# A graph network layer: layer 2 of the nodes computed with features on partitions, from layer 1's output split in two

## The chip, the cores and the metric

The kernel runs on one core of one Trainium2 chip. The metric is the device time of the whole program in microseconds (us), as the median of several runs. The engines are PE (TensorE, matrix products), DVE (VectorE), ACT (ScalarE), POOL (GpSimd) and SP (SyncE, which here only issues DMAs). Each runs its own instructions in program order and waits for the others by semaphores.

## The reference

There are 50000 nodes and 25000 edges, both with 128 features. Node rows are normalised and rectified to h. Each edge sends `[h[src], h[dst], edge features]` through a two-layer network (hidden width 256), the results are summed over the edges of each receiver, and each node sends `[h, sum]` through a second two-layer network whose output is added to x.

```
h = jnp.maximum(_layernorm(x, axis=-1), 0.0)
rel_inputs = jnp.concatenate([h[senders], h[receivers], relations], axis=-1)
rel_effects = relu(rel_inputs @ re_w1 + re_b1) @ re_w2 + re_b2
agg_effects = jax.ops.segment_sum(rel_effects, receivers, num_segments=h.shape[0])
effect_inputs = jnp.concatenate([h, agg_effects], axis=-1)
out = x + relu(effect_inputs @ ea_w1 + ea_b1) @ ea_w2 + ea_b2
```

The encoder with the weights oe_w1 and oe_w2 has no influence on the output, and the kernel leaves it out.

## The kernel before

Edges and nodes are worked in groups of 512 (G = 4 x 128, T = 4). There are 49 groups of edges, and 98 tiles of nodes that go in 49 pairs; r = 1 and r = 2 are the two tiles of a pair, j is the pair, e the group of edges. Edges come sorted by receiver, so the sum for a tile of nodes needs only a window of 128 edge results for each 128 nodes. The edges run three groups ahead of the nodes: three edge steps, then `enter`, then 46 joint steps (one group of edges and one pair of nodes each, e = 3 to 48, j = e - 3), then three pair steps with nodes alone.

A joint step does this. DVE takes statistics of the gathered rows of the next edge group and of the next x tiles (L726, L731), turns them into a scale and a shift (L738 to L758, with a square root by ACT in between, `deviations`), and normalises the edges' rows with eight 128x128 instructions (`normalise_edges`, L767); ACT normalises the nodes' rows (`normalise`, L638). PE transposes them to features on partitions (`turn_edges`, `turn_nodes`), and sums a window of edge results with a 0/1 matrix `hot` (`sum_window`), which DVE makes from the window (`mark`, L807). Everything that enters layer 1 is split in a high part, rounded to fp32r by ACT (`high_ea`, `high_edges`, `high_nodes`), and a low part, value minus high part, by DVE (`low_edges`, `low_features`, `low_sums`) or, for the edge features, by POOL (`low_ea`, L397). Layer 1 then takes for each of its two halves c of 128 hidden units the products high x w_high, high x w_low and low x w_high, as fp32r matmuls with 512 columns (L514, L519). ACT adds the bias and rectifies (`hidden`, L630). Layer 2 (L529) multiplies in plain fp32: for each of the four blocks of 128 rows, the hidden block stands still and the weights of 128 columns are moved through, twice, so the output has rows on partitions. DVE adds the bias and writes the edge results (`edge_results`), or adds `xb` = x + bias, which POOL has made (`keep_x`, L390), and writes the node results (`node_results`, L801). POOL also issues the gathers of the edges' rows: eight indirect DMAs a group (L374). SP loads windows, edge features and x tiles and stores the results.

The order on each engine is written out by hand in `joint_step` and `pair_step` of each engine's block; semaphores (`wait_ge`) hold an instruction until its inputs are there. The buffers l1_ps, l2_ps, node_ps and agg_ps are PSUM banks, the others lie in SBUF.

## Time and profile before

| | us |
|---|---|
| median of 3 runs | 969.56 (969.46 to 970.05) |
| the profiled execution, device time | 968.67 |
| its span (first to last instruction) | 966.9 |
| PE busy | 938.2 |
| DVE busy | 674.7 |
| POOL busy | 577.2 |
| ACT busy | 553.1 |

The profile is one execution. The span is 1.8 us shorter than the device time of the same execution, and the median of the runs is 0.9 us above that device time. In a row of a timeline the first number is the start from the span's begin, the second the duration, both in us; "x8" says that eight instructions stand in the row; the brackets say how long the engine had been idle before it and what ended that.

### The profile page before, as it was taken

The numbers are of one execution on the slowest core, as the hardware profiler recorded it, in microseconds if no ns is written. First come the engines' busy times: TensorE is split into PE (matmuls) and PEld (weight loads), VectorE is DVE, ScalarE is ACT, GpSimd is POOL, SyncE is SP. The second block draws the span as 40 slices with busy tenths as digits, with TensorE's granted clock in tenths as the row PEclk, the third lists the DMA queues.
The fourth block names the chain that finished last, engine by engine and source line by source line (L and its number), as shares of the span: only waits on it lengthen the run. The fifth ranks groups of instructions, "written<-read, shape, count | busy, mean of one in ns | idle before, by whom it ended". The sixth has DMA issues, their size and how long they took to land.

```text
span 966.9 us, 20070 instructions
## 1 busy us (share of the span) xinstructions
PE 938.2 (97%) x6058; PEld 834.2 (86%) x6058; DVE 674.7 (70%) x2057; ACT 553.1 (57%) x1082; POOL 577.2 (60%) x600
## 2 busy tenths in 40 slices
PE   4879999999999999999999999999999999999997
PEld 3668988998898898899889889988988998898886
DVE  5876776777677677767767776776776677677552
ACT  1356556556655655665565666566566556655653
POOL 7777666665665666566566656656665665662220
PEclk9999999999999999999999999999999999999999
DMA  6354444454544545454454545545444544543332
GB/s 197 91 130 114 138 139 137 144 145 133 159 144 133 143 143 146 131 158 143 131 151 143 142 129 156 146 128 164 134 143 125 157 144 129 164 138 117 109 91 70
DMA packets 114100, 132.51 MB, mean 137 GB/s; under 512 B 17984, under 2 KB 70080, under 8 KB 113984
## 3 DMA queue, kind: packets, MB, share of 16 engines
q1 hardware_dynamic: 101440, 105.43, 36.3%
q0 software_dynamic: 12544, 25.72, 10.6%
q8 instruction: 51, 0.84, 0.4%
q14 instruction: 65, 0.53, 0.2%
HBM read 92.07 MB, written 39.00 MB: 136 GB/s over the span
## 4 chain that ended last, share of the span: by engine, by line
PE 93%; DVE 4%; issue 1%; ACT 1%; DMA 0%; POOL 0%; SPq 0%; DVEq 0%; POOLq 0%
PE l_ps L514 32%; PE l_ps L529 27%; PE l_ps L519 16%; PE agg_ps L483 9%; PE edge_ps L467 4%; PE node_ps L475 4%; PE node_ps L459 1%; DVE h L767 1%; DVE st L726 1%; DVE st L731 0%; DVE hot L807 0%; DVE lo L774 0%; DMA gath<-in_x,dst_all 0%; DMA drow_i<-in_dst_rows 0%; POOL gath L374 0%
## 5 line engine op out<-in xcount | busy, mean ns | idle before, releaser
L374 POOL DMA_INDIRECT gath<-in_x,dst_all x196 | 193.6, 988 | 59.9 <-issue 59.9
L374 POOL DMA_INDIRECT gath<-in_x,src_all x196 | 188.1, 960 | 52.2 <-issue 45.8
L780 DVE SCALAR_TENSOR_TENSOR lo<-node_ps,hi 128x512 fp32r<-128x512 f32 x98 | 67.8, 692 | 202.7 <-ACT hi L621 202.7
L397 POOL TENSOR_TENSOR ea_lo<-ea_in,ea_hi 128x512 fp32r<-128x512 f32 x45 | 63.1, 1401 | 217.0 <-ACT ea_hi L612 217.0
L529 PE MATMUL l_ps<-w2n,hid 128*128 128x128 f32 x1568 | 190.9, 275 | 0.0
L529 PEld LDWEIGHTS l_ps<-w2n,hid 128*128 128x128 f32 x1568 | 183.0, 192 | 0.1
L630 ACT ACTIVATE hid<-l_ps,b1n 128x512 f32<-128x512 f32 x196 | 135.3, 690 | 81.9 <-PE l_ps L519 81.7
L638 ACT ACTIVATE h<-xin,shift,rs 128x128 f32<-128x128 f32 x392 | 165.0, 483 | 0.0
L514 PE MATMUL l_ps<-hi,w1n_hi 128*128 128x512 f32 x392 | 155.8, 398 | 0.6 <-ACT hid L630 0.6
L514 PE MATMUL l_ps<-hi,w1n_lo 128*128 128x512 f32 x392 | 155.4, 396 | 0.0
L390 POOL TENSOR_TENSOR xb<-xin,b2n 128x512 f32<-128x512 f32 x98 | 124.5, 1292 | 33.2 <-DVE res L801 33.2
L621 ACT ACTIVATE hi<-node_ps 128x512 fp32r<-128x512 f32 x98 | 58.2, 594 | 138.4 <-PE node_ps L475 138.2
L630 ACT ACTIVATE hid<-l_ps,b1e 128x512 f32<-128x512 f32 x98 | 67.7, 691 | 108.0 <-PE l_ps L519 108.0
L519 PE MATMUL l_ps<-lo,w1n_hi 128*128 128x512 f32 x392 | 123.6, 396 | 0.0
L483 PE MATMUL agg_ps<-hot,win 128*128 128x128 f32 x784 | 104.8, 277 | 3.6 <-DVE hot L807 3.4
L767 DVE TENSOR_SCALAR h<-gath,rs,shift 128x128 f32<-128x128 f32 x392 | 105.7, 344 | 1.8
L483 PEld LDWEIGHTS agg_ps<-hot,win 128*128 128x128 f32 x784 | 96.1, 193 | 4.7 <-issue 4.1
L529 PE MATMUL l_ps<-w2e,hid 128*128 128x128 f32 x784 | 95.9, 275 | 2.3 <-ACT hid L630 2.3
L529 PEld LDWEIGHTS l_ps<-w2e,hid 128*128 128x128 f32 x784 | 91.4, 192 | 3.6 <-ACT hid L630 3.6
L514 PEld LDWEIGHTS l_ps<-hi,w1n_hi 128*128 128x128 f32 x392 | 74.0, 189 | 19.2 <-ACT hid L630 1.4
L519 PEld LDWEIGHTS l_ps<-lo,w1n_hi 128*128 128x128 f32 x392 | 73.6, 188 | 18.2
L514 PEld LDWEIGHTS l_ps<-hi,w1n_lo 128*128 128x128 f32 x392 | 73.9, 189 | 17.4
(94 smaller groups left out, 1441.8 us busy)
## 6 DMA issues: line engine op xcount, KB each, us to landing
win<-rel_rows SPq DMA_DIRECT2D x392, 66.0 KB
xin<-in_x_tiles SPq DMA_DIRECT2D x98, 256.0 KB, 4.1
out<-res SPq DMA_DIRECT2D x98, 256.0 KB, 3.3
rel_rows<-rel_row SPq DMA_DIRECT2D x49, 264.0 KB
ea_in<-in_ea_t SPq DMA_DIRECT2D x49, 256.0 KB, 3.1
gath<-in_x,src_all POOLq DMA_INDIRECT x196, 2.7
gath<-in_x,dst_all POOLq DMA_INDIRECT x196, 2.6
w1e<-in_L_gnn_re_w SPq DMA_DIRECT2D x1, 384.0 KB
```

What stands on the lines that cost most here:

```text
L374: nc.gpsimd.indirect_dma_start(gath[b][:, s, k, :], None, x, bass.IndirectOffsetOnAxis(ap=idx[:, e * T + k:e * T + k + 1], axis=0)).then_i ...
L390: nc.gpsimd.tensor_tensor(xb[r][j % 2][:, :, :], xin[r][j % 3][:, :, :], b2[1][:, :].unsqueeze(1).to_broadcast([P, T, D]), ALU.add).then_i ...
L397: nc.gpsimd.tensor_tensor(ea_lo[e % 2][:, :], ea_in[e % 2][:, :], ea_hi[e % 2][:, :].bitcast(F32), ALU.subtract).then_inc(ea_lo_set, 1)
L483: last = nc.tensor.matmul(agg_ps[:, k * P:(k + 1) * P], win[r][:, k, 0:D], hot[r][:, k, :], start=True, stop=True)
L514: nc.tensor.matmul(l1_ps[c][:, :], part[:, q, c * P:(c + 1) * P], high, start=(i == 0 and part is w1hi[w]), stop=False)
L519: last = nc.tensor.matmul(l1_ps[c][:, :], w1hi[w][:, q, c * P:(c + 1) * P], low, start=False, stop=(i == len(srcs) - 1))
L529: last = nc.tensor.matmul(l2_ps[turn % 2][:, k * P:(k + 1) * P], hid[r][:, c, k * P:(k + 1) * P], w[:, c, :], start=(c == 0), stop=(c == C ...
L621: nc.scalar.activation(hi[r][:, 0, :], node_ps[:, :], ACT.Relu).then_inc(node_hi_set, 1)
L630: nc.scalar.activation(hid[r][:, c, :], l1_ps[c][:, :], ACT.Relu, bias=b[:, c:c + 1]).then_inc(hid_set, 1)
L638: last = nc.scalar.activation(h[r][:, k, :], xin[r][j % 3][:, k, :], ACT.Identity, bias=shift[j % 2][:, b:b + 1], scale=rs[j % 2][:, b:b + 1])
L767: last = nc.vector.tensor_scalar(h[0][:, s * T + k, :], gath[e % 2][:, s, k, :], rs[e % 2][:, t:t + 1], shift[e % 2][:, t:t + 1], ALU.mult ...
L780: nc.vector.scalar_tensor_tensor(out=lo[r][:, 0, :], in0=node_ps[:, :], scalar=0.0, in1=hi[r][:, 0, :].bitcast(F32), op0=ALU.max, op1=ALU. ...
```

## The change

Layer 2 of the nodes changes its form. The weights w2n stand still (128x128, one for each half c) and the hidden tile of 512 columns is moved through, so the output has features on partitions and 512 nodes as columns. It is done in split form, as layer 1 is. w2n and the hidden tile are split in high and low parts, and six fp32r matmuls of 512 columns take the place of eight plain fp32 ones of 128. ACT makes `hid_hi` with two copies a tile (`high_hidden`), POOL makes `hid_lo` with two subtractions a tile (`low_hidden`). The residual comes from a transposed copy of x, `x_t`, which SP loads for each tile (`load_xt`); the bias is now one number a partition, and `node_results` adds both in one instruction. `keep_x` and `xb` go. The output is stored in the transposed layout. x is still loaded in rows, for the statistics and the normalisation. Once, at the start, DVE splits w2n (`split_last_weights`). The order of the joint step changes on PE, ACT, DVE and POOL.

```diff
+            def layer2_nodes(r, j, turn):
+                wait(pe, results, turn - 1)
+                for c in range(C):
+                    pe.wait_ge(hid_hi_set, C * tile_no(r, j) + c + 1)
+                    nc.tensor.matmul(l2_ps[turn % 2][:, :], w2hi[:, c, :], hid_hi[r][:, c, :], start=(c == 0), stop=False)
+                    nc.tensor.matmul(l2_ps[turn % 2][:, :], w2lo[:, c, :], hid_hi[r][:, c, :], start=False, stop=False)
+                for c in range(C):
+                    pe.wait_ge(hid_lo_set, C * tile_no(r, j) + c + 1)
+                    last = nc.tensor.matmul(l2_ps[turn % 2][:, :], w2hi[:, c, :], hid_lo[r][:, c, :], start=False, stop=(c == C - 1))
```

The order of a joint step on PE:

```diff
             def joint_step(e, j):
-                for r, n in ((0, e), (1, j), (2, j)):
-                    for c in range(C):
-                        layer1(r, n, turn + r, c)
-                if j + 1 < NJ:
-                    turn_nodes(1, j + 1)
-                    sum_window(1, j + 1)
+                for r, n, c in ((0, e, 0), (0, e, 1), (1, j, 0), (1, j, 1), (2, j, 0)):
+                    layer1(r, n, turn + r, c)
+                turn_nodes(1, j + 1)
+                layer1(2, j, turn + 2, 1)
+                layer2(turn)
+                layer2_nodes(1, j, turn + 1)
                 if e + 1 < EG:
                     turn_edges(e + 1)
-                layer2(0, turn)
-                layer2(1, turn + 1)
-                if j + 1 < NJ:
-                    turn_nodes(2, j + 1)
-                    sum_window(2, j + 1)
-                layer2(2, turn + 2)
+                sum_window(1, j + 1)
+                layer2_nodes(2, j, turn + 2)
+                turn_nodes(2, j + 1)
+                sum_window(2, j + 1)
```

The new work of POOL:

```diff
+            def low_hidden(r, j):
+                for c in range(C):
+                    pool.wait_ge(hid_hi_set, C * tile_no(r, j) + c + 1)
+                    nc.gpsimd.tensor_tensor(hid_lo[r][:, c, :], hid[r][:, c, :], hid_hi[r][:, c, :].bitcast(F32),
+                                            ALU.subtract).then_inc(hid_lo_set, 1)
```

The new work of ACT, and its joint step as it stands now:

```diff
+            def hidden_nodes(r, j, turn, c):
+                act.wait_ge(l1_done, C * turn + c + 1)
+                wait(act, hid_lo_set, C * tile_no(r, j - 1) + c + 1)
+                nc.scalar.activation(hid[r][:, c, :], l1_ps[c][:, :], ACT.Relu, bias=b1[1][:, c:c + 1]).then_inc(hid_set, 1)
+
+            def high_hidden(r, j, turn, c, before):
+                act.wait_ge(hid_set, C * turn + c + 1)
+                if c == 0:
+                    wait(act, l2_done, before + 1)
+                nc.scalar.activation(hid_hi[r][:, c, :], hid[r][:, c, :], ACT.Copy).then_inc(hid_hi_set, 1)
...
             def joint_step(e, j):
+                normalise(1, j + 1, True)
                 if e + 1 < EG:
                     high_ea(e + 1, True)
+                hidden(turn, 0, before_edge(e, True))
+                hidden(turn, 1, before_edge(e, True))
+                hidden_nodes(1, j, turn + 1, 0)
+                deviations(e + 1, some(e + 1, EG), pair_of(e + 1))
+                hidden_nodes(1, j, turn + 1, 1)
+                for c in range(C):
+                    high_hidden(1, j, turn + 1, c, before_node(1, j, True))
+                hidden_nodes(2, j, turn + 2, 0)
+                high_features(1, j + 1)
+                high_hidden(2, j, turn + 2, 0, before_node(2, j, True))
+                hidden_nodes(2, j, turn + 2, 1)
+                high_hidden(2, j, turn + 2, 1, before_node(2, j, True))
+                normalise(2, j + 1, True)
                 if e + 1 < EG:
                     high_edges(e + 1)
+                high_sums(1, j + 1, True)
+                high_features(2, j + 1)
+                high_sums(2, j + 1, True)
```

The results of the nodes on DVE:

```diff
             def node_results(r, j, fast):
...
-                dve.wait_ge(xb_set[r], j + 1)
+                dve.wait_ge(xt_loaded[r][j % 3], 16 * (j // 3 + 1))
                 wait(dve, stored[r], 16 * j)
-                nc.vector.tensor_tensor(res[r][:, :, :], tiled(l2_ps[turn % 2]), xb[r][j % 2][:, :, :], ALU.add).then_inc(results, 1)
+                nc.vector.scalar_tensor_tensor(out=res[r][:, :], in0=l2_ps[turn % 2][:, :], scalar=b2[1][:, 0:1],
+                                               in1=xt[r][j % 3][:, :], op0=ALU.add, op1=ALU.add).then_inc(results, 1)
```

The order on POOL in one joint step before: after the eight gathers (the last of them is the first row), the low part of the next edge features, then x plus bias for both tiles of the next pair, then the marks of the edges' receivers (COPY) and the next gathers.

```order
L374 DMA gath<-in_x,dst_all 128x128
L397 TENSOR_TENSOR ea_lo<-ea_in,ea_hi 128x512 [waits ea_hi_set]
L390 TENSOR_TENSOR xb<-xin,b2n 128x512 [waits results,x_loaded12]
L390 TENSOR_TENSOR xb<-xin,b2n 128x512 [waits results,x_loaded22]
L384 COPY rel_row<-dst_f 128x4 [waits rel_stored0]
L374 DMA gath<-in_x,src_all 128x128 [waits normed0]
```

And the same place now.

```order
L396 DMA gath<-in_x,dst_all 128x128
L418 TENSOR_TENSOR ea_lo<-ea_in,ea_hi 128x512 [waits ea_hi_set]
L411 TENSOR_TENSOR hid_lo<-hid,hid_hi 128x512 [waits hid_hi_set] x4
L406 COPY rel_row<-dst_f 128x4 [waits rel_stored0]
L396 DMA gath<-in_x,src_all 128x128 [waits normed0]
```

Two additions for the next pair have become four subtractions for this pair, and each waits for ACT's `hid_hi`.

The order on DVE in the second part of one joint step before, from the scale and shift to the last low part.

```order
L801 TENSOR_TENSOR res<-l_ps,xb 128x512 [waits stored2,xb_set2,l2_done]
L756 RECIPROCAL rs<-sd 128x16 [waits deviation]
L758 SCALAR_TENSOR_TENSOR shift<-total,rs 128x16 [waits inverse]
L767 TENSOR_SCALAR h<-gath,rs,shift 128x128 [waits edges_turned,shift_set]
L767 TENSOR_SCALAR h<-gath,rs,shift 128x128 x7
L807 SCALAR_TENSOR_TENSOR hot<-node_no,win 128x512 [waits win_used1,win_loaded1]
L780 SCALAR_TENSOR_TENSOR lo<-node_ps,hi 128x512 [waits node_hi_set]
L785 TENSOR_TENSOR lo<-agg_ps,hi 128x512 [waits agg_hi_set]
L774 SCALAR_TENSOR_TENSOR lo<-edge_ps,hi 128x512 [waits edge_hi_set] x2
L793 TENSOR_TENSOR rel_row<-l_ps,b2e 128x4x128 [waits l2_done,rel_stored0]
L807 SCALAR_TENSOR_TENSOR hot<-node_no,win 128x512 [waits win_used2,win_loaded2]
```

And the same part now.

```order
L797 RECIPROCAL rs<-sd 128x16 [waits deviation]
L799 SCALAR_TENSOR_TENSOR shift<-total,rs 128x16 [waits inverse]
L849 SCALAR_TENSOR_TENSOR hot<-node_no,win 128x512 [waits win_used1,win_loaded1,shift_set]
L842 SCALAR_TENSOR_TENSOR res<-l_ps,b2n,xt 128x512 [waits stored2,xt_loaded21,l2_done]
L808 TENSOR_SCALAR h<-gath,rs,shift 128x128 [waits edges_turned]
L808 TENSOR_SCALAR h<-gath,rs,shift 128x128 x7
L849 SCALAR_TENSOR_TENSOR hot<-node_no,win 128x512 [waits win_used2,win_loaded2]
L834 TENSOR_TENSOR rel_row<-l_ps,b2e 128x4x128 [waits l2_done,rel_stored0]
L821 SCALAR_TENSOR_TENSOR lo<-node_ps,hi 128x512 [waits node_hi_set]
L842 SCALAR_TENSOR_TENSOR res<-l_ps,b2n,xt 128x512 [waits stored1,xt_loaded12,l2_done]
L815 SCALAR_TENSOR_TENSOR lo<-edge_ps,hi 128x512 [waits edge_hi_set] x2
L826 TENSOR_TENSOR lo<-agg_ps,hi 128x512 [waits agg_hi_set]
```

Both `hot` have moved: the first in front of the eight normalisations, the second right behind them, and the results and all low parts of the step stand behind that.

## Rows read from the trace of the kernel before

**Rows 1.** Windows, one joint step: length; PE, PEld, DVE, ACT, POOL busy; clock; DMA.
```profile
477.67:496.40 18.73, 18.73 (x125) 16.76 (x124) 13.42 (x43) 11.24 (x23) 11.82 (x13) 1.00 0.49 142
```
**Rows 2.** The chain that ended last, in that step: start, us, what.
```profile
482.13 0.94 PE l_ps L514 x4
...
487.75 0.44 PE node_ps L475 x4
488.19 0.89 PE agg_ps L483 x8
489.08 0.87 PE edge_ps L467 x8
489.95 3.57 PE l_ps L529 x32
```
**Rows 3.** Groups by line and form: busy us, mean ns of one, idle before.
```profile
L397 POOL TENSOR_TENSOR ea_lo<-ea_in,ea_hi 128x512 fp32r<-128x512 f32 x45 | 63.1, 1401 | 217.0 <-ACT ea_hi L612 217.0
...
L612 ACT ACTIVATE ea_hi<-ea_in 128x512 fp32r<-128x512 f32 x49 | 30.6, 626 | 2.7 <-DMA ea_in<-in_ea_t 2.7
...
L834 DVE TENSOR_TENSOR w1e_lo<-w1e,w1e_hi 128x768 fp32r<-128x768 f32 x1 | 1.0, 959 | 0.0
...
L832 DVE CAST w1e_hi<-w1e 128x768 fp32r<-128x768 f32 x1 | 0.6, 550 | 0.0
```
**Rows 4.** Timelines of that step, PE, ACT, DVE and POOL.
```profile
482.36 2.14 DVE L767 TENSOR_SCALAR h<-gath,rs,shift 128x128 f32<-128x128 f32 x8
...
483.37 0.39 PE L514 MATMUL l_ps<-hi,w1n_hi 128*128 128x512 f32 x1
...
483.57 0.69 ACT L630 ACTIVATE hid<-l_ps,b1n 128x512 f32<-128x512 f32 x1
...
484.86 1.39 POOL L397 TENSOR_TENSOR ea_lo<-ea_in,ea_hi 128x512 fp32r<-128x512 f32 x1 [4.64 <-ACT ea_hi L612]
...
486.22 2.53 POOL L390 TENSOR_TENSOR xb<-xin,b2n 128x512 f32<-128x512 f32 x2
...
489.02 1.00 POOL L374 DMA_INDIRECT gath<-in_x,src_all  x1
...
490.62 1.29 DVE L774 SCALAR_TENSOR_TENSOR lo<-edge_ps,hi 128x512 fp32r<-128x512 f32 x2 [0.18 <-ACT hi L617]
...
492.82 1.15 POOL L374 DMA_INDIRECT gath<-in_x,dst_all  x1 [0.30 <-issue]
```
**Rows 5.** Timelines of the first pair step: the square root and a DVE instruction after it.
```profile
928.50 0.30 ACT L606 ACTIVATE sd<-spread,eps 128x8 f32<-128x8 f32 x1 [1.48 <-DVE spread L750]
...
929.27 0.69 DVE L801 TENSOR_TENSOR res<-l_ps,xb 128x512 f32<-128x512 f32 x1
```
**Rows 6.** Timelines where POOL and DVE both work on SBUF tiles (behind `enter`; pair step).
```profile
56.56 2.50 POOL L390 TENSOR_TENSOR xb<-xin,b2n 128x512 f32<-128x512 f32 x2
...
57.70 1.91 DVE L807 SCALAR_TENSOR_TENSOR hot<-node_no,win 128x512 f32<-128x512 f32 x1
...
59.00 0.66 POOL L384 COPY rel_row<-dst_f 128x4 f32<-128x4 f32 x1
...
930.11 1.29 POOL L390 TENSOR_TENSOR xb<-xin,b2n 128x512 f32<-128x512 f32 x1 [4.44 <-DVE res L801]
...
930.82 1.12 DVE L807 SCALAR_TENSOR_TENSOR hot<-node_no,win 128x512 f32<-128x512 f32 x1 [0.85 <-DMA win<-rel_rows]
```
**Rows 7.** Instructions of one line: ns min/median/max, first and last start.
```profile
L767 DVE TENSOR_SCALAR h<-gath,rs,shift x392: 331/343/566, 20.3 to 896.3; 128x128 f32<-128x128 f32 x196
...
L801 DVE TENSOR_TENSOR res<-l_ps,xb x98: 683/692/692, 81.4 to 962.4; 128x512 f32<-128x512 f32 x98
...
L807 DVE SCALAR_TENSOR_TENSOR hot<-node_no,win x98: 677/682/1910, 57.7 to 949.4; 128x512 f32<-128x512 f32 x98
```
**Rows 8.** Just behind `enter`: a PE timeline row, and a window (columns as rows 1).
```profile
58.62 0.90 PE L475 MATMUL node_ps<-ident,h 128*128 128x128 f32 x4 [2.79 <-ACT h L638]
...
60.00:62.00 2.00, 2.00 (x11) 2.00 (x11) 0.69 (x1) 0.72 (x3) 1.70 (x2) 0.50 0.14 33
```

More of the change, by code:

```diff
@@ L113, in gnn_program @@
         xin = [None] + [[sb(f"xin{r}{b}", [P, T, D]) for b in range(3)] for r in (1, 2)]
-        xb = [None] + [[sb(f"xb{r}{b}", [P, T, D]) for b in range(2)] for r in (1, 2)]
+        xt = [None] + [[sb(f"xt{r}{b}", [P, G]) for b in range(3)] for r in (1, 2)]
+        hid_hi = [None] + [sb(f"hid_hi{r}", [P, C, G], F32R) for r in (1, 2)]
+        hid_lo = [None] + [sb(f"hid_lo{r}", [P, C, G], F32R) for r in (1, 2)]
         win = [None] + [sb(f"win{r}", [P, T, ROW]) for r in (1, 2)]
         hot = [None] + [sb(f"hot{r}", [P, T, P]) for r in (1, 2)]
-        res = [None] + [sb(f"res{r}", [P, T, D]) for r in (1, 2)]
+        res = [None] + [sb(f"res{r}", [P, G]) for r in (1, 2)]
         edge_ps = [ps(f"edge_ps{s}", [P, G]) for s in range(2)]
@@ L320, in _ @@
                     load_x(r, j)
+            for r in (1, 2):
+                load_xt(r, 0, True)
             def edge_step(e, last, fast):
@@ L343, in joint_step @@
                 for r in (1, 2):
+                    if j + 1 < NJ:
+                        load_xt(r, j + 1, True)
+                for r in (1, 2):
                     if j + 3 < NJ:
@@ L354, in pair_step @@
                     store(2, j - 1, fast)
+                for r in (1, 2):
+                    if j + 1 < NJ:
+                        load_xt(r, j + 1, fast)
                 for r in (1, 2):
@@ L427, in edge_step @@
                     gather(e + 2)
-                if last:
-                    pool.wait_ge(loaded[1], LOADS)
-                    for r in (1, 2):
-                        keep_x(r, 0, fast)
                 if FIRST < e + 1 < EG:
@@ L592, in pair_step @@
                     add(1, j + 1)
-                layer2(1, turn)
+                layer2_nodes(1, j, turn)
                 if j + 1 < NJ:
@@ L705, in pair_step @@
                     deviations(stats_turn(j + 2, fast), None, j + 2)
-                hidden(1, turn, 0, before_node(1, j, fast))
-                hidden(1, turn, 1, before_node(1, j, fast))
+                for c in range(C):
+                    hidden_nodes(1, j, turn, c)
+                    high_hidden(1, j, turn, c, before_node(1, j, fast))
                 if more:
                     normalise(2, j + 1, fast)
-                hidden(2, turn + 1, 0, before_node(2, j, fast))
-                hidden(2, turn + 1, 1, before_node(2, j, fast))
+                for c in range(C):
+                    hidden_nodes(2, j, turn + 1, c)
+                    high_hidden(2, j, turn + 1, c, before_node(2, j, fast))
                 if more:
@@ L894, in _ @@
             split_weights(1)
+            split_last_weights()
             def edge_step(e, last, fast):
@@ L923, in joint_step @@
                 spreads(*what)
+                invert(*what)
+                mark(1, j + 1)
                 if j > 0:
                     node_results(2, j - 1, True)
-                invert(*what)
                 if e + 1 < EG:
                     normalise_edges(e + 1, range(T))
-                if more:
-                    mark(1, j + 1)
-                    low_nodes(1, j + 1)
+                mark(2, j + 1)
+                edge_results(e, True)
+                low_features(1, j + 1)
+                node_results(1, j, True)
                 if e + 1 < EG:
                     low_edges(e + 1)
-                edge_results(e, True)
-                if more:
-                    mark(2, j + 1)
-                node_results(1, j, True)
-                if more:
-                    low_nodes(2, j + 1)
+                low_sums(1, j + 1)
+                low_nodes(2, j + 1)
             def pair_step(j, fast):
```

96 lines of the change are left out of this document (43 added, 53 removed).

## The prediction

> **What bounds the kernel now.** I read the windows first. In a joint step of the middle, PE is busy for 18.73 of 18.73 us, DVE for 13.42, ACT for 11.24, POOL for 11.82, and PE's granted clock is 1.00, which is 2.4 GHz [rows 1]. So PE sets the end, and 46 such steps make 862 of the 966.9 us. The chain that ended last says what PE does in it: a layer 1 matmul of 512 columns comes every 0.94 / 4 = 0.235 us, and layer 2 of two tiles of nodes takes 3.57 us, 1.79 a tile [rows 2]. The timelines then say what leaves room: POOL had been idle for 4.64 us before `low_ea`, and DVE's eight normalisations, begun at 482.36 and 2.14 us long, were over at 484.50, before POOL's first subtraction of the step began at 484.86 [rows 4]. In this kernel the two do not meet; that will matter.
>
> **What PE saves.** Layer 2 of a tile of nodes becomes six matmuls of 512 columns. Layer 1 has the same shape and type, so I take 6 x 0.235 = 1.41 us, 0.38 less than 1.79. A joint step becomes 18.73 - 0.75 = 17.98 us, if nothing waits. With nothing else, 98 tiles would give 37 us.
>
> **What the other engines get.** ACT gets four copies from SBUF of 0.63 us, priced by `high_ea` [rows 3]: 11.24 + 2.5 = 13.8 us, below 17.98. DVE gets nothing: the new `node_results` reads one PSUM and one SBUF tensor of 512, as the old one did at 0.69 [rows 7]. POOL loses two `xb` (2.53 together) and gets four subtractions of the form of `low_ea`, 1.39 in that step and 1.40 in the mean [rows 3, 4]. Its step was three gathers in 492.82 - 489.02 = 3.80 us, so 1.27 each; eight are 10.2, the COPY about 0.3, five subtractions 7.0, together 17.5 us. That is under 17.98, but only just. SP gets two more loads of the size of those of x a step; the 16 DMA engines are busy for 0.49 of the time [rows 1], and a fifth more bytes leave them under 0.6. I take 0 for it, as the loads are issued a step ahead. At the start `split_last_weights` adds two small DVE instructions, about 0.6 us, and the additions of `keep_x` that held up DVE's first `hot` (1.91 instead of 0.68 us [rows 6, 7]) go, 1.2 us: together -0.6.
>
> **Where the work now stands in a step.** I lay the new order out from t = 0, PE's first matmul of the step, with 0.235 a matmul and the 0.44, 0.87 and 0.89 of [rows 2]. PE: both halves of layer 1 of the edges end at 4.2, tile 1 at 5.6 and 7.0, tile 2's half 0 at 8.5, transposes 8.9, half 1 at 10.3, layer 2 of the edges 12.1, of tile 1 at 13.5, `turn_edges` 14.4, window sum 15.3, layer 2 of tile 2 at 16.7, transposes 17.1, window sum 18.0. ACT starts on a result 0.20 after PE has gone on [483.57 against 483.37, rows 4]: `hidden_nodes` of tile 1, half 0, at 5.8, then the square root at 6.4, half 1 at 7.25, `high_hidden` at 7.85, done at 8.5. The later `hid_hi` are done by my count at 9.1, 10.8 and 12.1. POOL, whose gathers and `low_ea` are over by about 7.9, therefore subtracts at 8.5, 9.9, 11.2, 12.6, back to back until 14.0. DVE: 0.77 us after the start of the square root it is free for the next instruction [rows 5], so `hot` of tile 1 at 7.2, `node_results` of tile 2 at 7.8 and the eight normalisations from 8.4 (instructions of 512 follow each other every 0.60, the pair of 1.29 less one of 0.69 [rows 4, 7]). Unhindered they end at 10.5, three us before PE wants them at 13.5. **They now fall upon POOL's four subtractions.**
>
> **What such a meeting costs.** `hot`, which reads two SBUF tensors, met an `xb` of POOL twice. At 57.70 it took 1.91 us instead of 0.68 and ended at 59.61, 0.55 behind the end of POOL's pair at 59.06; at 930.82 it took 1.12 and ended at 931.94, 0.54 behind POOL's end [rows 6]. Streaming 512 elements takes about that, so DVE did not start until POOL had finished: one waits for the whole instruction of the other. It is mutual: the COPY of 0.2 us issued at 59.00 took 0.66. `node_results`, which has one input in PSUM, was never above 0.692 [rows 7]. The normalisation has one SBUF input and an SBUF output. A cast of such a form does 768 elements in 0.55 us where a subtraction of two tensors takes 0.96 [rows 3], so this form moves twice as many in the same time and must use both of DVE's ways into SBUF. And while its median is 343 ns, one took 566 [rows 7], during a gather's index read. I therefore take it that it waits for a subtraction as `hot` does. Its price lies between nothing (its longest delay shown is 0.22) and the whole subtraction each time POOL has one.
>
> A page gives the rule: the Trainium skill, SBUF — State Buffer, section "Who interferes with whom", says that a DVE instruction in a two-port mode (a tensor_scalar can run so) or with two SBUF inputs and a GpSimd instruction exclude each other for whole instructions. For `hot` the trace agrees (1.91 and 1.12 us); for the normalisation no row has the meeting.
>
> **The sum.** One normalisation slips in at the end of each subtraction, which the COPY's turn at 59.06 speaks for. Four are then done when POOL ends, at about 14.3 with the hand-overs; four more at 0.26 lead to 15.4. Behind them stand in order the second `hot`, `edge_results`, `low_features`, `node_results`, two `low_edges` and `low_sums`: the seventh starts 6 x 0.60 later, at 19.0, and ends at 19.7. PE's last window sum waits for it, since agg_ps has to be read before: 19.8 to 20.7, and with the restart 20.8 us a step. PE's own waits are about 1.3 us at `turn_edges` and 1.5 before that last sum. The excess is 20.8 - 18.73 = 2.07 us in each of the 45 steps that still normalise edges, 93 us. The last joint step has none: -0.8 for PE, about +1 for a `hot` that waits for POOL, so 0. The three pair steps put four ACT copies of about 0.6 in front of `high_features`, for which PE waits there, and save 0.75: about +1 each for the two with a successor, +2. The start: -0.6. The span is 966.9 + 93 + 2 - 0.6 = 1061.3. The device time was 1.8 longer, and the median 0.9 above that: 1064 us.
>
> **The rivals.** (a) **POOL keeps its turn.** At 57.83, between the two `xb`, the waiting `hot` did not get in. Then no normalisation passes until 14.0, eight end at 16.2, the last low part at 20.5, the step is 21.5: 45 x 2.8 = 125 us, 1096. (b) **Two pass at each hand-over**, as they are pipelined (0.26 apart, 0.34 long): 0.9 us less a step, 1024. (c) **The normalisation does not mind POOL**, on the other side: what decides is whether its form takes POOL's way into SBUF at all. Then DVE is 0.8 us free before each need, the steps are 18.0, and 46 x 0.75 = 34.5 us are gained: 966.9 - 34.5 + 2 - 0.6 + 2.7 = 937. Against it stand the cast's speed and the 566 ns. (d) **DVE goes first and keeps its turn**, starting at 8.4, just before POOL: POOL begins at 11.2, the second `hid_lo` is there at 13.9 where PE wants it at 13.3, and the step is 18.6: 963 to 967. Against it: POOL's index read came in between two normalisations. (e) **The clock.** After a PE idle stretch of 2.79 us the granted clock of the window 60 to 62 was 0.50, 1.2 GHz [rows 8]. If the waits of a step bring that, some 4 us at half speed cost 2 us more a step: about 1155. The new single waits are about half as long, so this is unlikely. (f) The matmuls cost more than in layer 1: same shape, same types, I give it nothing.
>
> **How the numbers follow.** Chances: forecast 0.47, (a) 0.24, (b) 0.09, (c) 0.12, (d) 0.05, (e) 0.03. The cases forecast, (a) and (b) hold 0.80; their range, with 4 us for my rounding, is 1020 to 1100. About 0.2% (2 us) is what a measurement here can tell from no change. Faster: (c) and part of (d), 0.14; within 0.2%: 0.03; slower: 0.83.
>
> **What would show it.** Right: normalisations of some 1.4 us beside subtractions that follow without a gap; PE idle at `turn_edges` and before the second window sum of a step, released by DVE; joint steps of about 20.8 us; layer 2 of a tile at 1.41 us. Wrong: normalisations that keep 0.34 us (then 937), or a clock below 1.00 in joint steps (then far above 1100).

## The result and the profile after

The changed kernel takes **1028.84 us** (median of 4 runs, 1027.49 to 1032.22) where the kernel before, on the same chip, takes 969.51 (968.68 to 970.05). The ratio is 1.0618, with a 95% interval of 1.059 to 1.0646: 6% slower. The forecast was 1064, its range 1020 to 1100. The profiled execution of the changed kernel spans 1025.6 us, 58.7 more than the 966.9 of before.

From the page of the changed kernel: busy times, the chain that ended last, and two groups, in the form of [rows 3].

```profile
PE 933.6 (91%) x5078; PEld 764.8 (75%) x5078; DVE 847.3 (83%) x2059; ACT 644.9 (63%) x1278; POOL 690.5 (67%) x698
...
PE 49%; DVE 32%; issue 15%; ACT 3%; POOL 0%; DMA 0%; DVEq 0%; SPq 0%; POOLq 0%; ACTq 0%
...
L411 POOL TENSOR_TENSOR hid_lo<-hid,hid_hi 128x512 fp32r<-128x512 f32 x196 | 247.2, 1291 | 201.0 <-ACT hid_hi L670 200.5
...
L808 DVE TENSOR_SCALAR h<-gath,rs,shift 128x128 f32<-128x128 f32 x392 | 291.2, 812 | 0.1
```

The normalisation took 344 ns in the mean before (343 in the median [rows 7]) and now takes 812 in the mean, and DVE, which had 4% of the chain before, has 32%. One joint step of the middle, as [rows 1] and with the same columns:

```profile
482.06:502.00 19.94, 18.67 (x105) 15.30 (x104) 17.21 (x41) 13.07 (x26) 14.04 (x14) 1.00 0.56 161
```

18.73 us have become 19.94, at a granted clock of 1.00. The timelines of that step, DVE, POOL and PE, in place of [rows 4]:

```profile
490.64 6.31 DVE L808 TENSOR_SCALAR h<-gath,rs,shift 128x128 f32<-128x128 f32 x8
...
490.64 5.01 POOL L411 TENSOR_TENSOR hid_lo<-hid,hid_hi 128x512 fp32r<-128x512 f32 x4 [3.60 <-ACT hid_hi L670]
...
496.69 0.68 DVE L849 SCALAR_TENSOR_TENSOR hot<-node_no,win 128x512 f32<-128x512 f32 x1
...
500.34 0.67 DVE L826 TENSOR_TENSOR lo<-agg_ps,hi 128x512 fp32r<-128x512 f32 x1
...
494.10 0.47 PE L552 MATMUL l_ps<-hid_hi,w2n_hi 128*128 128x512 f32 x1
...
495.56 1.18 PE L482 MATMUL edge_ps<-ident,h 128*128 128x128 f32 x6
...
497.01 0.44 PE L482 MATMUL edge_ps<-ident,h 128*128 128x128 f32 x2 [0.26 <-DVE h L808]
...
497.29 1.06 PE L498 MATMUL agg_ps<-hot,win 128*128 128x128 f32 x8
...
499.58 0.60 PE L490 MATMUL node_ps<-ident,h 128*128 128x128 f32 x4
...
501.12 1.13 PE L498 MATMUL agg_ps<-hot,win 128*128 128x128 f32 x8 [0.94 <-issue]
```

The first two rows of PE say what the change gave: layer 2 of a tile runs from 494.10 to 495.56, 1.46 us in place of 1.79. The rest says what it took. Eight normalisations last 6.31 us where they lasted 2.14, beside four subtractions of POOL. In the whole run 179 of the 392 normalisations take more than 1.2 us, four in nearly every one of the 45 joint steps that have them. PE stands idle for them at `turn_edges` (0.26 in its row, and more between the transposes that the row merges) and before the step's last window sum (0.94). The profile calls that second wait `issue`; by the code, `sum_window` waits there for the last low part of DVE, which is over at 501.01. Cut into narrower windows, the 6.31 us read so:

```profile
490.64 1.37 DVE L808 TENSOR_SCALAR h<-gath,rs,shift 128x128 f32<-128x128 f32 x1
...
491.93 2.55 DVE L808 TENSOR_SCALAR h<-gath,rs,shift 128x128 f32<-128x128 f32 x2
...
494.41 1.59 DVE L808 TENSOR_SCALAR h<-gath,rs,shift 128x128 f32<-128x128 f32 x2
...
495.66 0.59 DVE L808 TENSOR_SCALAR h<-gath,rs,shift 128x128 f32<-128x128 f32 x2
```

They start at 490.64, 491.93, 493.18 and 494.41, one every 1.25 us, which is the spacing of the subtractions (5.01 / 4). From 495.66, when POOL is done, they come 0.26 apart. Two more rows, of the line of the normalisation (ns min/median/max) and of who waited for it (us, times):

```profile
L808 DVE TENSOR_SCALAR h<-gath,rs,shift x392: 329/524/1389, 20.6 to 954.9; 128x128 f32<-128x128 f32 x196
...
  PEld edge_ps L482: 36.2, 93
```

So PE's weight loads wait 0.8 us a step (36.2 / 45) inside `turn_edges`; the 0.26 of the PE row lies within that. What the two places cost is read from the starts of the rows. `turn_edges` runs from 495.56 to 497.29, 1.73 us, and the last window sum starts 1.54 us behind the start of `turn_nodes` (499.58 to 501.12). The kernel without POOL's subtractions (x3_no_sub, below) has 0.87 and 0.53 us there. The differences, 0.86 and 1.01, and that kernel's step of 18.06 make 19.93: the step.

**Where the 58.7 us lie.** The step of e = 3 starts at 64.20 (before: 64.73), the last joint step at 960.48 (before: 908.53). The start gives back 0.5; 45 steps of 19.92 instead of 18.75 cost 52.5. From there to the last result of DVE it is 57.21 instead of 54.52, +2.7. And behind the last result comes a stretch of 7.9 us instead of 3.9. Of the kernel before and of the one after, the last row of the chain and the row of the instruction with which POOL's queue ends:

```profile
962.36 0.69 DVE L801 TENSOR_TENSOR res<-l_ps,xb 128x512 f32<-128x512 f32 x1 [1.09 <-PE l_ps L529]
```
```profile
L44 POOLq DRAIN  x1: 7667/7667/7667, 944.4 to 944.4; - x1
```
```profile
1016.94 0.75 DVE L842 SCALAR_TENSOR_TENSOR res<-l_ps,b2n,xt 128x512 f32<-128x512 f32 x1 [1.17 <-PE l_ps L556]
```
```profile
L44 POOLq DRAIN  x1: 7666/7666/7666, 1017.7 to 1017.7; - x1
```

POOL's drain takes 7.67 us. Before, it began at 944.4 and was over at 952.1, long before the end. Now POOL works until the last layer 2, the drain begins at 1017.7, and the program ends 0.2 us behind it. That is +4.1 us that the forecast did not have; x11_end_on_dve, below, tests it. -0.5 + 52.5 + 2.7 + 4.1 is 58.8.

### The profile page after: what moved, and what is told of

It is laid out like the page before. It is cut to its first block, busy times and chain, and to the rows that moved or that the text cites. A ratio compares the mean times of both kernels' runs of the same rounds, so it can differ in the third digit from the quotient of the medians.

```text
span 1025.6 us, 18464 instructions
## 1 busy us (share of the span) xinstructions
PE 933.6 (91%) x5078; PEld 764.8 (75%) x5078; DVE 847.3 (83%) x2059; ACT 644.9 (63%) x1278; POOL 690.5 (67%) x698
## 2 busy tenths in 40 slices
DMA packets 128208, 158.05 MB, mean 154 GB/s; under 512 B 19680, under 2 KB 71648, under 8 KB 128096
## 4 chain that ended last, share of the span: by engine, by line
PE 49%; DVE 32%; issue 15%; ACT 3%; POOL 0%; DMA 0%; DVEq 0%; SPq 0%; POOLq 0%; ACTq 0%
DVE h L808 23%; PE l_ps L529 18%; PE agg_ps L498 10%; PE l_ps L534 9%; DVE res L842 3%; PE l_ps L552 2%; PE l_ps L556 2%; PE l_ps L553 2%; PE edge_ps L482 2%; PE node_ps L490 2%; ACT sd L630 1%; DVE rs L797 1%; DVE shift L799 1%; DVE st L772 1%; DVE st L767 1%
## 5 line engine op out<-in xcount | busy, mean ns | idle before, releaser
L411 POOL TENSOR_TENSOR hid_lo<-hid,hid_hi 128x512 fp32r<-128x512 f32 x196 | 247.2, 1291 | 201.0 <-ACT hid_hi L670 200.5
L808 DVE TENSOR_SCALAR h<-gath,rs,shift 128x128 f32<-128x128 f32 x392 | 291.2, 812 | 0.1
L396 POOL DMA_INDIRECT gath<-in_x,dst_all x196 | 185.9, 949 | 59.7 <-issue 59.7
L529 PE MATMUL l_ps<-hi,w1n_hi 128*128 128x512 f32 x392 | 159.7, 407 | 1.8 <-ACT hid L664 1.8
L678 ACT ACTIVATE h<-xin,shift,rs 128x128 f32<-128x128 f32 x392 | 160.6, 482 | 0.0
L826 DVE TENSOR_TENSOR lo<-agg_ps,hi 128x512 fp32r<-128x512 f32 x98 | 66.9, 683 | 64.5 <-ACT hi L653 64.5
L670 ACT ACTIVATE hid_hi<-hid 128x512 fp32r<-128x512 f32 x196 | 118.2, 628 | 1.9
L641 ACT ACTIVATE hi<-edge_ps 128x512 fp32r<-128x512 f32 x98 | 53.2, 595 | 102.2 <-PE edge_ps L482 102.2
L653 ACT ACTIVATE hi<-agg_ps 128x512 fp32r<-128x512 f32 x98 | 59.1, 603 | 74.8 <-PE agg_ps L498 74.8
L482 PE MATMUL edge_ps<-ident,h 128*128 128x128 f32 x392 | 74.3, 292 | 14.1 <-DVE h L808 10.1
```

The source lines that it names most:

```text
L396: nc.gpsimd.indirect_dma_start(gath[b][:, s, k, :], None, x, bass.IndirectOffsetOnAxis(ap=idx[:, e * T + k:e * T + k + 1], axis=0)).then_i ...
L411: nc.gpsimd.tensor_tensor(hid_lo[r][:, c, :], hid[r][:, c, :], hid_hi[r][:, c, :].bitcast(F32), ALU.subtract).then_inc(hid_lo_set, 1)
L482: last = nc.tensor.transpose(edge_ps[s][:, k * P:(k + 1) * P], h[0][:, s * T + k, :], ident[:, :])
L529: nc.tensor.matmul(l1_ps[c][:, :], part[:, q, c * P:(c + 1) * P], high, start=(i == 0 and part is w1hi[w]), stop=False)
L670: nc.scalar.activation(hid_hi[r][:, c, :], hid[r][:, c, :], ACT.Copy).then_inc(hid_hi_set, 1)
L678: last = nc.scalar.activation(h[r][:, k, :], xin[r][j % 3][:, k, :], ACT.Identity, bias=shift[j % 2][:, b:b + 1], scale=rs[j % 2][:, b:b + 1])
```

## The experiments

The theory: DVE's normalisation and POOL's subtraction shut each other out for whole instructions, one normalisation passes at each hand-over, and that chain delays the last low part of the step. The rivals left are that something else of the change (traffic, matmuls, ACT's copies) costs the time, and that the interference follows another rule. Unless something else is said, each kernel is the changed one with the edit shown; the kernel before took 968.96 to 970.49 us beside them.

**Without the subtractions**

```diff
-                for r in (1, 2):
-                    low_hidden(r, j)          # and layer 2 reads hid_hi in the place of hid_lo
```

> The changed kernel without POOL's four subtractions a joint step (and four a pair step); the last two matmuls of layer 2 of a tile read hid_hi in place of hid_lo, so the low part of the hidden tile is left out of the result. PE, ACT, DVE and DMAs keep their order. Theory (DVE's normalisations of the edges wait for POOL's subtractions, one passing per subtraction): the eight normalisations fall from 6.3 us a step to 2.1, joint steps from 19.94 us to about 18.0, the span from 1025.6 to 1025.6 - 45 x 1.95 = 938. Rival (the new order on the engines, or the waits of ACT and PE for one another, make the steps long): normalisations short, but steps still above 19.5 us, span above 1010. Rival (memory traffic of the second copy of x): span unchanged within 3 us.

942.21 us, ratio 0.9721 [0.9701, 0.974]. POOL's subtractions and the waits of PE and ACT for them are the only thing that is left out (the output lacks the low part of the hidden tile). A joint step as in [rows 1], the line of the normalisation, and the PE rows of the two places:

```profile
481.87:499.93 18.06, 18.06 (x105) 15.33 (x104) 13.56 (x42) 13.07 (x26) 9.49 (x11) 1.00 0.60 176
```
```profile
L805 DVE TENSOR_SCALAR h<-gath,rs,shift x392: 328/342/585, 20.3 to 871.6; 128x128 f32<-128x128 f32 x196
```
```profile
495.36 1.04 PE L480 MATMUL edge_ps<-ident,h 128*128 128x128 f32 x8
...
496.23 1.06 PE L496 MATMUL agg_ps<-hot,win 128*128 128x128 f32 x8
...
498.52 0.60 PE L488 MATMUL node_ps<-ident,h 128*128 128x128 f32 x4
...
499.05 1.13 PE L496 MATMUL agg_ps<-hot,win 128*128 128x128 f32 x8
```

The step is 18.06 us, all of it PE, and the normalisation has its 342 ns again. That is 0.08 over the forecast's 17.98, with the matmuls, ACT's copies, the new `res` and the loads all in it: they do not make a joint step longer, and the 1.9 us are the subtractions. It is not PE's wait for `hid_lo` itself either: in the changed kernel PE waits for it once in the whole run, 0.3 us, near the end.

**Without the loads of x_t**

```diff
             def load_xt(r, j, fast):
                 if j > 2:
-                    sp.wait_ge(results, node_turn(r, j - 3, fast) + 1)
+                    return
```

> The changed kernel without the loads of x in the second layout (x_t) from the fourth pair of tiles on: node_results adds old values, and 92 of the 98 loads of 256 KB are left out. It prices the traffic that the change adds. My theory (the step is set by POOL's subtractions and DVE's normalisations between them, the loads are hidden): joint steps stay at 19.9 us, profiled span 1025.6 +- 3 us, time about 1029. The rival (the added bytes slow the gathers, and with them the edges): the steps fall by some tenths of a us, the span to 1020 or below.

1028.54 us (1027.55 to 1029.53), ratio 1.0593 [1.055, 1.0636]. Bytes moved fall from 158.05 to 133.91 MB, the span is 1027.7, and the last window sums of steps start at 901.98, 921.91, 941.84 and 961.78, still 19.93 apart. The traffic is hidden.

**The subtractions cut in two, and joined in pairs**

```diff
-                    nc.gpsimd.tensor_tensor(hid_lo[r][:, c, :], hid[r][:, c, :], hid_hi[r][:, c, :].bitcast(F32), ...
+                    for f in (slice(0, G // 2), slice(G // 2, G)):                       # x4_halves
+                        last = nc.gpsimd.tensor_tensor(hid_lo[r][:, c, f], hid[r][:, c, f], ...
...
-                for c in range(C):                                                           # x5_double, once a tile
+                pool.wait_ge(hid_hi_set, C * tile_no(r, j) + C)
+                nc.gpsimd.tensor_tensor(hid_lo[r][:, :, :], hid[r][:, :, :], ...
```

> The changed kernel with each of POOL's subtractions cut in two of 256 columns. Theory (one normalisation passes at the end of each POOL instruction): eight ends in place of four, so all eight normalisations are through when POOL is; POOL's work grows to about 5.3 us, the second hot starts 5.3 us after the first normalisation and not 6.05, steps of about 19.2 us, span about 990. Rival (a fixed delay by the time that POOL works, whatever the number of its instructions): the second hot starts later by what POOL's work grows, span 1030 to 1045.

> The changed kernel with the two subtractions of a tile made one of 1024 columns. Theory (one normalisation passes at the end of each POOL instruction): the first subtraction starts 0.5 us later, at 9.1 us of the step, so two or three normalisations are through before; it lasts about 2.3 us; four or five remain and the second subtraction starts about 0.4 us behind the first one's end, so about three stay behind it until 14.3 us: second hot at about 15.0 instead of 14.6 us, steps of 20.1 to 20.4 us, span 1030 to 1045. Rival (a fixed price per POOL instruction or per hand-over): half as many of them, steps shorter than now, span below 1010.

1008.4 us (1008.18 to 1008.62), ratio 1.0403 [1.0383, 1.0424], and 1045.61 (1045.38 to 1045.83), ratio 1.0759 [1.072, 1.0799]. The rows of x4_halves, then of x5_double:

```profile
483.07 5.24 DVE L810 TENSOR_SCALAR h<-gath,rs,shift 128x128 f32<-128x128 f32 x8
...
482.63 5.60 POOL L412 TENSOR_TENSOR hid_lo<-hid,hid_hi 128x256 fp32r<-128x256 f32 x8 [2.27 <-ACT hid_hi L672]
...
478.80 1.62 DVE L781 TENSOR_TENSOR total<-st 128x32 f32<-128x32 f32 x1
...
479.06 1.29 POOL L420 TENSOR_TENSOR ea_lo<-ea_in,ea_hi 128x512 fp32r<-128x512 f32 x1
```
```profile
479.58 5.50 DVE L807 TENSOR_SCALAR h<-gath,rs,shift 128x128 f32<-128x128 f32 x5
...
479.40 2.51 POOL L410 TENSOR_TENSOR hid_lo<-hid,hid_hi 128x1024 fp32r<-128x1024 f32 x1 [3.88 <-ACT hid_hi L669]
...
482.27 2.47 POOL L410 TENSOR_TENSOR hid_lo<-hid,hid_hi 128x1024 fp32r<-128x1024 f32 x1 [0.36 <-ACT hid_hi L669]
```

The same elements are subtracted in all three. With halves the price of a normalisation is that of one instruction of POOL: 5.24 / 8 = 0.66 us beside 5.60 / 8 = 0.70. With double ones, the individual normalisations show one held for 2.41 us beside each of POOL's two instructions, and six that pass before, between and behind them (between them POOL waits 0.36 us for ACT). So each instruction of POOL holds one normalisation for its whole length, long or short. The eight together last 6.27 us, no more than with single ones; that fewer and longer subtractions lengthen the chain is not shown. The steps of x5_double alternate between 20.07 and 20.51 us, with the second `hot` at 14.75 and 15.20 us of the step, where the changed kernel has 14.63.

Part of both results is another meeting: `total`, a DVE instruction of 0.20 us on two small SBUF tiles, met `low_ea` and took 1.62 us. It did so in nearly every step of x4_halves and in every other step of x5_double, the longer ones, and it delays the first normalisation, to 9.0 us of the step instead of 8.6. That is what was off for the halves, where I wanted steps of 19.2 us and a span of about 990: the second `hot` came 5.16 us behind the first normalisation, for 5.3 forecast, but the steps were 19.50 us and the span 1006.7.

**The subtractions on DVE**

```diff
+                low_hidden(1, j)              # now in DVE's code, ahead of edge_results
                 edge_results(e, True)
+                low_hidden(2, j)
                 low_features(1, j + 1)
```

> The changed kernel with the four subtractions of the hidden tile done by DVE in place of POOL (0.6 us each there, 2.4 us a step). Theory: DVE has 13.4 + 2.4 = 15.8 us of work in a step of 18.0, and nothing of POOL meets the normalisations but low_ea, which ends before; steps of 18.0 to 18.5 us, span 938 to 962. Rival (DVE is the engine that is short, whoever delays it): DVE's chain from the square root to low_sums is 1.2 to 2.4 us longer than without the subtractions, so steps of 18.8 to 19.8, span 975 to 1020.

955.97 us (954.94 to 957.49), ratio 0.9868 [0.9851, 0.9884]. With nobody on the other side, the rows of a step have 2.13 us for eight normalisations and 1.29 for two subtractions, which follow each other every 0.6 us on DVE, where POOL needs 1.25. Steps are about 18.3 us; DVE's longer queue holds up the last sum by 0.22.

**The square root and the normalisations early (x1_early)**

```diff
+                deviations(e + 1, some(e + 1, EG), pair_of(e + 1))    # ACT, ahead of hidden_nodes(1, j, turn + 1, 0)
                 invert(*what)
+                if e + 1 < EG:
+                    normalise_edges(e + 1, range(T))                  # DVE, ahead of mark and node_results
                 mark(1, j + 1)
```

> The changed kernel with the edges' normalisations moved out of the way: ACT takes the square root before hidden_nodes of tile 1, half 0, and DVE normalises the edges before hot and node_results. Nothing is left out, POOL's four subtractions stay. Theory: the normalisations start about 6.4 us into the step and end at 8.5, where POOL begins; hot of tile 2 waits for one subtraction at most, with no one waiting for it; steps of 18.0 to 18.3 us, span 938 to 952, so faster than the kernel before. Rival (POOL's subtractions slow the step for another reason, as that POOL has no time left: its step was counted at 17.3): steps of 19 us or more, span 980 or more.

1048.8 us (1045.7 to 1049.38), ratio 1.0822 [1.0804, 1.084]: a miss, and slower than the changed kernel. Every other step is as expected, 18.05 us (471.10 to 489.15). The one after it takes 22.87:

```profile
489.15:512.02 22.87, 19.91 (x106) 16.66 (x104) 18.82 (x42) 13.18 (x26) 18.44 (x19) 0.93 0.49 139
```
```profile
495.26 1.61 DVE L799 SCALAR_TENSOR_TENSOR shift<-total,rs 128x16 f32<-128x16 f32 x1
...
495.53 1.30 POOL L418 TENSOR_TENSOR ea_lo<-ea_in,ea_hi 128x512 fp32r<-128x512 f32 x1
...
496.91 6.14 DVE L808 TENSOR_SCALAR h<-gath,rs,shift 128x128 f32<-128x128 f32 x8
...
497.72 4.99 POOL L411 TENSOR_TENSOR hid_lo<-hid,hid_hi 128x512 fp32r<-128x512 f32 x4 [0.89 <-ACT hid_hi L670]
...
504.36 0.77 PE L552 MATMUL l_ps<-hid_hi,w2n_hi 128*128 128x512 f32 x1 [2.96 <-DVE res L842]
```

`shift`, 16 columns wide and 0.17 us long by itself, met `low_ea` and took 1.61. The normalisations, late by that, fell on the subtractions after all; `node_results` stood behind them, and PE waited 2.96 us for the free PSUM bank and went on at a lower granted clock (0.93 in the mean of the step). An order with a margin of a microsecond failed on the smallest instruction in it.

**The same, with low_ea behind the subtractions (x8_early_ea_last, and once more as x8_again)**

```diff
-                if e + 1 < EG:
-                    low_ea(e + 1)
                 for r in (1, 2):
                     low_hidden(r, j)
+                if e + 1 < EG:
+                    low_ea(e + 1)
```

> x1_early with one more change: POOL makes the low part of the next edge features behind the four subtractions of the hidden tiles and not ahead of them (PE wants it 1.6 us into the next step). Nothing is left out. Theory (x1 failed because shift, a DVE instruction with two SBUF inputs, met low_ea and took 1.61 us, which pushed the normalisations back into the subtractions): shift and the normalisations now fall in a stretch where POOL has no tensor instruction, shift takes 0.2 and the eight normalisations 2.1 to 2.4 us, the first starts at 6.5 us of the step; steps of 18.0 to 18.3 us, span 938 to 952. Rival (x1 was slow because hot and node_results came later, for which PE waited, or because POOL has no time left): steps above 19.5 us, span above 1000.

946.3 us (945.48 to 947.4), ratio 0.9741 [0.9712, 0.977].

```profile
479.72:497.79 18.07, 18.07 (x106) 15.34 (x104) 13.93 (x42) 13.19 (x26) 14.80 (x15) 1.00 0.58 176
```
```profile
485.83 0.18 DVE L799 SCALAR_TENSOR_TENSOR shift<-total,rs 128x16 f32<-128x16 f32 x1
...
486.05 2.14 DVE L808 TENSOR_SCALAR h<-gath,rs,shift 128x128 f32<-128x128 f32 x8
...
488.30 5.82 POOL L411 TENSOR_TENSOR hid_lo<-hid,hid_hi 128x512 fp32r<-128x512 f32 x4 [0.98 <-ACT hid_hi L670]
```

One move on POOL beside x1_early makes 102 us: `shift` has its 0.18, the normalisations 2.14 and are over 0.1 before POOL begins, and every step is PE's 18.07. All of the new layer 2 is kept here, subtractions on POOL included: the loss was one of order, not of work. This version beats both kernels.

**DVE with the subtractions and the early square root (x9_dve_early)**

```diff
 x2_on_dve, and:
+                deviations(e + 1, some(e + 1, EG), pair_of(e + 1))    # ACT, as in x1_early
+                high_features(1, j + 1)       # ACT, pair step, ahead of the copies of tile 2
```

> x2_on_dve (subtractions of the hidden tiles on DVE) with the square root ahead of hidden_nodes of tile 1 on ACT, and in the pair steps the high features of tile 1 ahead of the copies of tile 2. Nothing is left out. Theory: DVE's chain starts 0.9 us earlier, so the last low part is there before PE's last window sum wants it; steps go from 18.3 to about 18.0 us, 46 x 0.25 = 11 us, and the pair steps give 1 to 2 us: span 938 to 942. Rival (x2 was bound by POOL or DMA): unchanged within 3 us of 953.

954.91 us (953.16 to 956.34), ratio 0.982 [0.9789, 0.9851], where I wanted 938 to 942. A miss: the step stays at 18.28, because the square root is not what DVE's last low part hangs on.

```profile
480.91 0.69 DVE L836 TENSOR_TENSOR rel_row<-l_ps,b2e 128x512 f32<-128x512 f32 x1 [0.86 <-PE l_ps L534]
...
496.69 2.48 POOL L396 DMA_INDIRECT gath<-in_x,dst_all  x1 [0.30 <-issue]
```

`edge_results` waits 0.86 us for PE, and seven instructions of 0.6 stand behind it. The second row is a gather, otherwise 0.94, that met two subtractions of DVE.

**The pair steps of the best version (x10_best)**

```diff
                 for c in range(C):
                     hidden_nodes(2, j, turn + 1, c)
+                if more and fast:
+                    high_features(1, j + 1)
+                for c in range(C):
                     high_hidden(2, j, turn + 1, c, before_node(2, j, fast))
```

> The version with the square root early, the normalisations ahead of hot and node_results and low_ea behind the subtractions, and in the pair steps ACT's high_features of tile 1 ahead of the copies of tile 2's hidden layer. In the changed kernel PE waited 1.78 us for ACT in the first pair step, and a pair step took 13.95 us instead of 13.1 to 13.4. Only the two pair steps with a successor can gain: joint steps 18.07 us as without the tweak, pair steps about 13.0 us, so 1 to 2 us less than 946.3: 944 to 946 us, ratio to the kernel before 0.973. Rival: PE waits next for something else in those steps (the copies of tile 2, which now end later), and the time stays at 946 to 947.

946.77 us (945.41 to 948.84), ratio 0.9758 [0.9729, 0.9787]: no change, as the rival had it. PE's waits of 1.39 for ACT and 1.27 for `hot` in the first pair step become one of 2.33 for `hot`, since `low_sums`, ahead of `hot` on DVE, now waits for ACT's later copy.

**The end of the program**

```diff
             def pair_step(j, fast):           # POOL, in x8_early_ea_last
+                if j < NJ - 1:
                     for r in (1, 2):
                         low_hidden(r, j)      # those of the last pair go to DVE, behind node_results(2, j - 1)
```

> The version with the square root early, the normalisations ahead of hot and node_results and low_ea behind the subtractions, once more, beside the next kernel on the same chip. Its profile had DVE's last result at 935.85 and its end at 943.7 us: 7.85 us behind it, where the kernel before has 3.85 (963.05 and 966.9). I expect 945 to 947 us again.

> The same version with the four subtractions of the last pair of tiles on DVE, which is idle for 6.24 us there. Theory: what lies behind the last result is POOL's DRAIN at the end of the program, which takes 7.67 us from the moment POOL's queue is empty; in the kernel before it begins at 944.4 and is hidden, in the changed kernel and in this version it begins at DVE's last result, since POOL's last subtraction ends just before. With the last subtractions on DVE, POOL is done one pair step earlier: the drain begins before 922 us, the stretch behind the last result falls from 7.85 to 3.9 to 4.3 us, and PE's wait of 0.25 us for the last hid_lo goes. Span 939.5 +- 0.7, time 941.5 to 943, some 4 us below the run beside it. Rival: the stretch is the store of out in its new layout (128 rows of 2 KB), or the profile's own; then it stays at 7.9 us and the time falls by at most 0.5 us.

947.42 us (947.29 to 948.63) without the edit and **943.28** (941.48 to 943.58) with it, on the same chip; ratios to the kernel before 0.9771 [0.975, 0.9792] and 0.972 [0.9698, 0.9742]. Drain and last result, without and with:

```profile
L44 POOLq DRAIN  x1: 7667/7667/7667, 937.6 to 937.6; - x1
```
```profile
936.79 0.75 DVE L842 SCALAR_TENSOR_TENSOR res<-l_ps,b2n,xt 128x512 f32<-128x512 f32 x1 [1.16 <-PE l_ps L556]
```
```profile
L44 POOLq DRAIN  x1: 7688/7688/7688, 925.0 to 925.0; - x1
```
```profile
935.71 1.55 DVE L849 SCALAR_TENSOR_TENSOR res<-l_ps,b2n,xt 128x512 f32<-128x512 f32 x2
```

The stretch behind the last result falls from 945.5 - 937.54 = 8.0 us to 941.2 - 937.26 = 3.9. The drain it was; the store in its new layout, which both have, costs nothing. This is the fastest version tried, 2.8% below the kernel before.

**The other way round: the kernel before with an early high_ea (x6_before_early_ea)**

```diff
+                if e + 1 < EG:
+                    high_ea(e + 1, True)      # ACT, in the kernel before, ahead of hidden(0, turn, 0, ...)
                 hidden(0, turn, 0, before_edge(e, True))
```

> The kernel before with one instruction moved: ACT makes ea_hi of the next edges ahead of hidden of the edges, so POOL's low_ea and its two xb follow its gathers at once and fall beside DVE's normalisations. Theory: the normalisations, 0.34 us each at present, take up to 1.3 us there, the eight together 3.3 to 5 us instead of 2.1, as POOL's xb (no hidden tile, no new layout) hold them up too; PE wants them 6 us later, so the span stays within 2 us of 966.9. Rival (only the new subtractions or the new order lengthen them): eight in 2.1 to 2.3 us.

It was to bring the old `xb` upon the normalisations and got 975.42 us (973.49 to 977.57), ratio 1.0045 [1.0025, 1.0066]. In the steady steps it missed: the normalisations kept 2.14 us, what was hit was `shift`, and PE did not notice (18.73 us). At the start it met them once. The profiled span is 975.5 us, 8.6 more than before where I wanted at most 2, and nearly all of that lies there: the step of e = 3 starts at 69.41 (before: 64.73) and takes 22.95 us (before: 19.55). Rows of a steady step, then of the start:

```profile
490.91 1.27 DVE L758 SCALAR_TENSOR_TENSOR shift<-total,rs 128x16 f32<-128x16 f32 x1
...
490.86 1.28 POOL L390 TENSOR_TENSOR xb<-xin,b2n 128x512 f32<-128x512 f32 x1 [1.34 <-DVE res L801]
...
56.32 4.03 DVE L767 TENSOR_SCALAR h<-gath,rs,shift 128x128 f32<-128x128 f32 x4
...
57.76 2.49 POOL L390 TENSOR_TENSOR xb<-xin,b2n 128x512 f32<-128x512 f32 x2
```

Four normalisations lasted 4.03 us, where the kernel before has 1.36 at that place; one of them alone took 3.26, through the end of a gather and both `xb`. What the rest of the lost time at the start is, is not shown. So an addition of POOL shuts them out as a subtraction does, and here POOL was not interrupted between two instructions. Why, where `low_hidden` lets one pass each time, is open. `low_hidden` checks a semaphore before each subtraction, but so does `keep_x` before each `xb`.

## Why the prediction was right, and where it was off

**What PE saves**: right. 1.46 us a tile instead of 1.41, and a step of 18.06 us without the meeting (x3_no_sub) for 17.98.

**Where the work stands**: right to 0.2 us. From the step's start at 482.06 the square root came at 6.5 (forecast 6.4), and normalisations and subtractions both began at 8.6 (8.4 and 8.5).

**What a meeting costs**: the mechanism is right. x3_no_sub and x8_early_ea_last show that the meeting is the cost, x4_halves and x5_double that a normalisation is held for one instruction of POOL, whatever its length. One passes at each hand-over, as the individual rows have it. That refutes (a), POOL keeps its turn, for this step, (b), two pass, (c), no meeting, and (d), DVE goes first. Rival (b) named 1024 us, nearer to the result than my own number, but for a reason that the rows contradict. The rule of the Trainium skill (SBUF — State Buffer, "Who interferes with whom"), that the two shut each other out for whole instructions, agrees with the measured 1.25 us for each normalisation. The range reached down to the result only because it held rival (b): my own case with the 4 us for rounding would have begun at 1060. That far, the result's place in the range is luck.

**The mis-sized term** is the length of the meeting. I took 1.39 us for a subtraction, from `low_ea` [rows 4], as if it stood alone, and added something for hand-overs. But `low_ea` began at 484.86, inside a `hot` that reads two SBUF tensors and ended at 485.11:

```profile
484.42 0.69 DVE L807 SCALAR_TENSOR_TENSOR hot<-node_no,win 128x512 f32<-128x512 f32 x1
```

It does so in 44 of its 45 cases, and the 1393 ns of its median are 1294 in x6_before_early_ea, the same kernel with `low_ea` at another place of the step. So my price held a meeting already. Back to back the subtractions come 1.25 us apart, and the hand-over is free: the normalisation that passes lies inside. [rows 4] had the right figure too, two `xb` in 2.53, 1.27 each. So POOL ended at 13.6 us of the step, not 14.3, the second `hot` came at 14.6, not 15.4, the last low part was done at 18.95, not 19.7, and the step is 19.94, not 20.8. PE's waits were forecast at 1.3 and 1.5 us and are 0.86 and 1.01. Each tenth counts 45 times: 52.5 us instead of 93.

**The last steps**: 0 and +2 forecast, +2.7 measured. PE waits 1.78 us in the first pair step for ACT's `hid`, which stands behind the square root there and not behind the copies that I had named; those cost 1.18 in the second pair step (`high_features`).

**The missing term**: POOL's drain, +4.1 us. I gave POOL work in the last layer 2 and looked only at who waits for its results, not at what its queue has left to do when it is done.

**The start**, -0.6 forecast, -0.5 measured. The first `hot` has its 0.68 us again, as forecast, but the step of e = 3 starts anywhere from 64.0 to 65.2 us in the profiles of the changed kernel's versions, so the half microsecond bears nothing out. **The clock** stayed at 1.00 in the joint steps, where PE's longest idle stretch was 1.01 us, so (e) did not come. In x1_early, with one of 2.96, it fell to 0.93 in the mean of the step. And in the first pair step of the changed kernel, behind the 1.78 us, a window shows it at its lower level (columns as [rows 1]); the layer 1 matmuls there come 0.43 apart instead of 0.23, part of the +2.7:

```profile
984.00:986.00 2.00, 2.00 (x6) 1.51 (x6) 0.00 (x0) 2.00 (x6) 1.89 (x2) 0.50 0.55 145
```

The sum was thus 94 us where 59 came. The two errors were of opposite sign (41 too much, 4 too little).

## What to carry to other kernels

Before work goes to GpSimd, look at what VectorE does in those microseconds: here an instruction of VectorE with two SBUF inputs, or a normalisation from SBUF to SBUF, however small, waited until the GpSimd instruction beside it ended, and a chain of eight such paid 4.2 us a step for 5.0 of GpSimd's. Try the order first: three moves gave 82 us here, the work moved to VectorE 73, and GpSimd instructions of half the length 20. Price back-to-back instructions by the spacing of a merged row, and look whether the one that you take the price from had met something itself. And let GpSimd finish early: its drain of 7.67 us at the end of the program is free only if something else takes longer.

## What the hardware showed that I had not expected

- VectorE instructions of 16 to 32 columns with two SBUF inputs pay the full price of a meeting: `shift`, 0.17 us, became 1.61, and `total`, 0.20 us, became 1.62. `BATCH_NORM_STATS2` and the results that read PSUM were never lengthened in the changed kernel: `res`, with one input in PSUM and one in SBUF, took 731 to 752 ns in all 98 cases.
- It works the other way too: a gather of 0.94 us took 2.48 beside two subtractions of VectorE (x9_dve_early).
- The same holds for an elementwise instruction of POOL: `low_ea` took 1393 ns in the median in the kernel before, where it began inside a `hot`, and 1294 to 1302 in x6_before_early_ea and in the changed kernel, where it began beside `BATCH_NORM_STATS2`. The forecast counted that tenth of a microsecond four times a step.
- POOL's drain at the end of the program takes 7.65 to 7.69 us in every kernel here.
